# The first two rows of a Sobel stage: row gradients made by VectorE instead of TensorE, and the loads cut to suit

## The chip, the core and the metric

The kernel runs on one core of a Trainium2 chip. Times are device microseconds (us) of that core for one launch of the whole program. A core has a matrix unit (TensorE, PE in the profile, its weight loads PEld), a vector unit (VectorE, DVE), an activation unit (ScalarE, ACT), a general unit (GpSimd, POOL) and a unit that mostly issues DMA transfers (SyncE, SP). ScalarE and GpSimd issue transfers too. Each engine works through its own list of instructions in order, and semaphores tie the lists together.

## The reference, cut to what matters

A batch of 16 images of 3 x 256 x 256 is turned into tokens by a Sobel filter; one attention layer and one feed-forward layer follow. The change touches the first step alone:

```python
kx, ky = _sobel_kernels()   # 3 x 3, per channel
Ix = _dwconv(x, kx)
Iy = _dwconv(x, ky)
G = jnp.hypot(Ix, Iy)
return jnp.sum(G, axis=1)   # over the 3 channels
```

With image rows a, b, c one above the other, and 0, 1, 2 for a shift by that many columns, an output row of `Iy` is `(a0 + 2 a1 + a2) - (c0 + 2 c1 + c2)` and an output row of `Ix` is `(a2 - a0) + 2 (b2 - b0) + (c2 - c0)`. Only their absolute values matter, since `hypot` follows.

## The kernel before, in words

The images go through the core in four groups of four (`GB = 4`). A group fills 128 partitions: 32 partitions for an image, and each partition holds 8 rows of it (`ROWS = 8`), with two more rows below for the filter, in the buffer `img`. "Row r" is thus row r of every partition, 128 x 768 numbers (3 channels x 256 columns), and one instruction on it covers a 32nd of each image. The rows are worked off in pairs (`PAIRS = 4`).

For groups 1 to 3 VectorE makes both gradients itself, in `magnitude_rows`, in between the attention and feed-forward work of the group before. Group 0 has no earlier group beside it. There TensorE makes the gradients, in `stencil(r)`, as sums in its accumulators (`psum`): each term is a matrix product of the identity, or of the identity times -1 or -2 (`ident`, `nident`, `n2ident`), with a row of the image or with a helper row. VectorE makes the helper rows: `edge` = `2 a1 + a0` of an image row, and `lead` = `2 b2 - a0`. `stencil(r)` makes gy from four terms, then gx from five, each term as a product of 512 columns and one of 256; each product of these 4-byte numbers shows in the trace as two instructions, so a term reads "x4". `magnitudes(i)` on ScalarE takes the absolute values of a pair out of the accumulators into `mag_y` and `mag_x`. Then VectorE and ScalarE together run `hypotenuse` on the pair, some fifty VectorE instructions that begin with the maximum and the minimum of the two magnitudes, row by row (f = 0 and 1). Between its steps a hook, `feed`, makes the helper rows of the next pair (`stencil_inputs`), so that TensorE works one pair ahead. `feed` waits for `img_in`, the semaphore of all image rows of the group.

`Chain` (the `u` of the code) orders dependent instructions on VectorE: with `lag=1` an instruction waits until the one before the last is done; `u.all()` waits for all that went before.

The order of the start is written out by hand. SyncE issues the loads of rows 0 to 3 of images 0 and 2, then the table of constants `cst`, then rows 4 to 9 of all images, then weights. ScalarE issues the loads of rows 0 to 3 of images 1 and 3. A load is one transfer per image and channel. VectorE waits for the table, scales the identity by -1 and -2, waits for `img_first` (rows 0 to 3 of all four images), and makes edge 0, edge 2, lead 0, edge 1, edge 3, lead 1. TensorE waits for both scaled identities and for the helper rows it needs. After the last row of group 0 SyncE loads the images of group 1; it knows that by the count of `stencil_psum`, 16 before.

Lines of the kernel before in the profile: L375 issues the image loads and L394 the table; L822 scales the identity; L531 is every `scalar_tensor_tensor` on VectorE (`stt`), L528 every `tensor_tensor` (`tt`), L525 the masking; L1527 is a term of gy and L1539 a term of gx on TensorE; L1266 and L1268 are the absolute values of gy and gx; L1228 is the first square of `hypotenuse` on ScalarE and L1232 the reciprocal root. `edge` and the temporaries `tmp` lie in the big buffers that the profile calls "arena"; `lead` lies in "xT", `nident` and `n2ident` in "onehot".

Of the kernel before, what the change touches and what calls it, by code (L numbers as in the profile page):

```python
# [21 lines left out]
ALU = mybir.AluOpType  # L22
# [99 lines left out]
def tower_kernel(nc, x, cls_tok, w_in, b_qk, b_v, w_out, b_out, w1, conv_w, conv_b, w2, const, out):  # L122
# [9 lines left out]
    with ExitStack() as ctx:  # L132
# [174 lines left out]
        img_first = sem("img_first")  # L307
# [79 lines left out]
        def _(sp):  # L387
# [122 lines left out]
        def _(dve):  # L510
# [296 lines left out]
            def stencil_inputs(rows):  # L807

                for r in rows:
                    if r >= 2:  # L810
                        dve.wait_ge(stencil_psum, 2 * r - 3)
                    edge_row(edge[:, (r + 2) % 4], r + 2).then_inc(edges_out, 1)
                    if r >= 2:
                        dve.wait_ge(stencil_psum, 2 * r - 2)
                    stt(lead[:, r % 2], px(r + 1, 2), 2.0, px(r, 0), ALU.mult, ALU.subtract).then_inc(leads_out, 1)

            def first_group(u):


                dve.wait_ge(table_in, 16)  # L820
                for k, out_ in ((-1.0, nident), (-2.0, n2ident)):
                    v.tensor_scalar(out_, ident, k, None, ALU.mult).then_inc(negated, 1)  # L822
                dve.wait_ge(img_first, FIRST_IN)
                for r in range(2):
                    edge_row(edge[:, r], r).then_inc(edges_out, 1)
                    stencil_inputs([r])
                for i in range(PAIRS):
                    def feed(k, i=i):
                        if k == 1 and i < PAIRS - 1:
                            if i == 0:  # L830
                                dve.wait_ge(img_in, IMG_IN)
                            stencil_inputs((2 * i + 2, 2 * i + 3))
                    hypotenuse(u, 2 * i, i, feed, [mag_x[:, f] for f in range(2)], [mag_y[:, f] for f in range(2)])
# [327 lines left out]
        def _(act):  # L1161
# [96 lines left out]

            def magnitudes(i):

                for f in range(2):
                    r = 2 * i + f
                    if i > 0:
                        act.wait_ge(hisq, 2 * i)
                    act.wait_ge(stencil_psum, 2 * r + 1)
                    s.activation(mag_y[:, f], stencil_sum(2 * r % 4), ACT.Abs).then_inc(mags_y, 1)  # L1266
                    act.wait_ge(stencil_psum, 2 * r + 2)
# [188 lines left out]
            for b in range(1, GB, 2):  # L1456
                load_rows(act, 0, b, 0, 4, img_first)
            act.wait_ge(table_in, 16)
            for i in range(PAIRS):
                magnitudes(i)  # L1460
# [46 lines left out]
        def _(pe):  # L1507
# [7 lines left out]
            def stencil(r):  # L1515
# [3 lines left out]
                if r >= 2:  # L1519
                    pe.wait_ge(mags_y, r - 1)  # L1520
# [8 lines left out]
                pe.wait_ge(leads_out, r + 1)  # L1529
                if r >= 2:  # L1530
                    pe.wait_ge(mags, r - 1)
# [12 lines left out]
            for r in range(ROWS):  # L1544
                if r == 2:
                    pe.wait_ge(img_in, IMG_IN)
# [277 lines left out]
```

## Time and profile before

| | |
|---|---|
| median of 3 runs | 1623.98 us (1623.11 to 1624.61) |
| the profiled execution, its own time | 1622.37 us |
| its span (first to last instruction) | 1620.3 us |
| VectorE busy | 1373.8 us, 85% |
| TensorE busy | 839.6 us, 52% |
| ScalarE busy | 699.8 us, 43% |
| GpSimd busy | 110.1 us, 7% |
| mean granted TensorE clock | 0.707 of full speed |

The span is what the trace covers; the run's own time is 2.1 us longer. In the timelines an entry gives its start and its length in us, and "x3" says that three like instructions were merged into it. What stands in brackets is how long the engine was idle just before it, and who released it.

### The profile page before, as it was taken

Reading aid. Unit: us, or ns where it says so; the run is one execution under the profiler, and the core shown is the slowest. Engines: PE = TensorE matmul, PEld = TensorE weight load, DVE = VectorE, ACT = ScalarE, POOL = GpSimd, SP = SyncE. Lnnn points to the kernel's source line nnn. Section 1 sums busy time; section 2 is a strip of 40 time slices with the busy share of each in tenths; the row PEclk is TensorE's granted clock in tenths of the full one; section 3 lists DMA queues with packets and bytes.
Section 4 is the critical chain, followed back from the end, with each engine's and each line's share of the span. In section 5 each row is a group of like instructions: output and inputs, shape, how many; then the busy total and the mean of one; then the engine's idle time right before and its main releaser. Section 6 shows DMA issues by size and latency. Waiting matters only on the chain.

```text
span 1620.3 us, 12694 instructions
## 1 busy us (share of the span) xinstructions
PE 839.6 (52%) x3318; PEld 655.5 (40%) x3318; DVE 1373.8 (85%) x2145; ACT 699.8 (43%) x1250; POOL 110.1 (7%) x154
## 2 busy tenths in 40 slices
PE   6663200466447743456537754256626764388543
PEld 3332100355336532344426543145525643376433
DVE  1999998899879999899879999899888999722676
ACT  1312332364375544164356553245446653132562
POOL 0000000001101000002101100002010100000000
PEclk9777655766569876667568976577568886577776
DMA  7000500013303510104302610104120300100001
GB/s 192 1 13 14 111 0 0 1 20 52 62 10 59 112 39 1 29 1 71 59 13 41 129 39 1 28 1 72 32 40 10 62 12 28 27 1 0 1 0 27
DMA packets 33421, 57.15 MB, mean 35 GB/s; under 512 B 6410, under 2 KB 23354, under 8 KB 31674
## 3 DMA queue, kind: packets, MB, share of 16 engines
q0 software_dynamic: 21024, 29.11, 11.1%
q1 hardware_dynamic: 12026, 26.31, 7.1%
q10 hardware_dynamic: 288, 0.79, 0.2%
q8 instruction: 32, 0.52, 0.1%
q14 instruction: 51, 0.42, 0.1%
HBM read 22.84 MB, written 4.25 MB: 17 GB/s over the span
## 4 chain that ended last, share of the span: by engine, by line
DVE 30%; issue 26%; ACT 15%; PE 12%; DMA 1%; DVEq 0%; ACTq 0%; SPq 0%
DVE arena L531 9%; DVE arena L528 6%; PE psum L1722 2%; ACT arena L1273 2%; DVE arena L872 2%; PE psum L1672 2%; PE psum L1694 1%; PE psum L1723 1%; PE psum L1576 1%; DVE red L544 1%; PE psum L1758 1%; ACT arena L1409 1%; ACT arena L1169 1%; DVE others L531 1%; ACT zT L1418 1%
## 5 line engine op out<-in xcount | busy, mean ns | idle before, releaser
L528 DVE TENSOR_TENSOR arena<-arena 128x768 f32<-128x768 f32 (+2 forms) x534 | 486.7, 967 | 45.8 <-ACT arena L1207 23.1
L531 DVE SCALAR_TENSOR_TENSOR arena<-arena 128x768 f32<-128x768 f32 (+2 forms) x224 | 201.4, 948 | 0.1
L1590 PE MATMUL psum<-zT,w1q 128*128 128x257 f32 x512 | 150.1, 431 | 41.8 <-ACT wout L1303 25.2
L1590 PEld LDWEIGHTS psum<-zT,w1q 128*128 128x128 f32 x512 | 111.3, 220 | 68.1 <-issue 27.5
L1576 PE MATMUL psum<-gpad,win 128*128 128x257 f32 x288 | 86.0, 442 | 54.9 <-ACT gpad L1285 54.9
L1238 ACT ACTIVATE arena<-arena 128x768 f32<-128x768 int16 x32 | 27.0, 843 | 175.6 <-DVE arena L531 175.2
L1694 PE MATMUL psum<-arena 128*128 128x257 f32 x128 | 50.6, 563 | 86.5 <-ACT arena L1392 65.3
L1576 PEld LDWEIGHTS psum<-gpad,win 128*128 128x128 f32 x288 | 62.6, 223 | 71.9 <-ACT gpad L1285 61.0
L531 DVE SCALAR_TENSOR_TENSOR arena<-img 128x768 f32<-128x768 f32 x88 | 79.5, 949 | 7.0 <-issue 6.4
L504 POOL DMA_DIRECT2D h<-others x60 | 51.7, 862 | 416.6 <-DVE others L531 347.7
L1169 ACT ACTIVATE arena<-arena 128x256 f32<-128x256 f32 x65 | 23.3, 409 | 118.4 <-DVE arena L531 68.2
L1694 PEld LDWEIGHTS psum<-arena 128*128 128x128 f32 x128 | 34.4, 282 | 98.0 <-issue 83.7
L872 DVE TENSOR_REDUCE arena<-arena 128x288 f32<-128x2304 f32 (+1 forms) x16 | 64.6, 4093 | 0.1
L1722 PE MATMUL psum<-arena 128*128 128x64 f32 x256 | 56.5, 361 | 12.3 <-ACT arena L1392 12.3
L476 POOL DMA_DIRECT2D arena<-nrows_mem x18 | 15.6, 902 | 695.1 <-ACT arena L1217 532.1
L1382 ACT ACTIVATE arena<-psum,arena 128x257 f32<-128x257 f32 x64 | 29.5, 474 | 72.5 <-DVE arena L971 72.5
L1292 ACT ACTIVATE xT<-psum,cb 128x257 f32<-128x257 f32 x96 | 43.5, 477 | 36.3 <-PE psum L1576 36.1
L531 DVE SCALAR_TENSOR_TENSOR arena<-arena,others 128x768 f32<-128x768 int16 x64 | 58.2, 950 | 0.0
L1722 PEld LDWEIGHTS psum<-arena 128*128 128x128 f32 x256 | 48.8, 262 | 19.6 <-ACT arena L1392 13.9
L1273 ACT ACTIVATE arena<-xT 128x2048 f32<-128x2048 f32 (+1 forms) x14 | 55.3, 3948 | 0.3
L1647 PE MATMUL psum<-xT,win 128*128 128x257 f32 x128 | 50.2, 559 | 8.4 <-issue 6.9
L531 DVE SCALAR_TENSOR_TENSOR arena<-arena,small 128x256 f32<-128x256 f32 x131 | 53.3, 480 | 0.6
(222 smaller groups left out, 1993.5 us busy)
## 6 DMA issues: line engine op xcount, KB each, us to landing
img<-x SPq DMA_DIRECT2D x36, 258.0 KB, 7.0
h<-others POOLq DMA_DIRECT2D x60, 128.0 KB, 2.7
arena<-nrows_mem POOLq DMA_DIRECT2D x18, 384.0 KB, 4.4
arena<-arena POOLq DMA_DIRECT2D x18, 384.0 KB, 4.1
arena<-img POOLq DMA_DIRECT2D x18, 384.0 KB, 4.9
out<-out SPq DMA_DIRECT2D x16, 256.0 KB
img<-x SPq DMA_DIRECT2D x48, 64.5 KB, 7.7
win<-w_in SPq DMA_DIRECT2D x4, 768.0 KB, 5.4
```

Source lines behind the costliest of these rows:

```text
L504: pool.dma_start(h9[:, row, :], others[:, row % 2, c, :], accum_op=ALU.add).then_inc(row_sums, 16)
L528: return v.tensor_tensor(o, a, b, op)
L531: return v.scalar_tensor_tensor(out=o, in0=a, scalar=s, in1=b, op0=op0, op1=op1)
L872: return v.tensor_reduce(fmax[:, :, bass.ds(b, 1), :].rearrange("p j o r -> p j (o r)"), f4[:, :, :, bass.ds(b, 1), :].rearrange("p t j o ...
L1169: ins = s.activation(ln[1][:, j, :], src(j), ACT.Square)
L1273: s.activation(fb[:, :, 0:ROWS, :], yd[:, :, 1:S].rearrange("p t (r j) -> p t j r", j=ROWS), ACT.Silu)
L1292: s.activation(ydw[:, t, :], (C0, C1, T0, T1)[i % 4][:, 0:S], ACT.Identity, bias=cb[:, t:t + 1]).then_inc(conv_taken, 1)
L1576: ins = mm((C0, C1, T0, T1)[i % 4][:, 0:S], diagonal(t, k), gpad[:, i % 4, k:k + S], start=(k == 0), stop=(k == 2))
L1590: ins = mm((A0, A1, B0, B1)[i % 4][:, 0:S], w1q[:, k, t * P:(t + 1) * P], zT[:, k, b, :], start=(k == 0), stop=(k == DT - 1))
L1647: ins = mm((A0, A1)[t][:, 0:S], win[:, k, D + t * P:D + (t + 1) * P], xT[:, k, b, :], start=(k == 0), stop=(k == DT - 1))
L1694: mm((C0, C1, T0, T1)[hg][:, 0:S], qbd[:, hg // 2, 4 * (hg % 2):4 * (hg % 2) + 4, :].rearrange("p h q -> p (h q)"), kT[:, b % 2, hg // 2, ...
L1722: mm(B1[:, chans], attnT[:, f, m, cols], V[:, b % 2, m, chans], start=(m == 0), stop=False)
```

## The change

For rows 0 and 1 of group 0 the gx of both and the gy of row 1 are made by VectorE in a new function, `first_gradients`, from the image rows in `img` and the helper rows. TensorE makes only gy of row 0, and goes on with row 2 (`stencil(0)` returns after gy). ScalarE takes absolute values in place for what VectorE made (`first_magnitudes`), and scales the identity, which VectorE did before. The loads of rows 0 to 3 are cut in two: rows 0 to 2 of all images first (`img_first`), and row 3 by transfers of its own (`img_second`), after the table on SyncE's queue. `first_gradients` waits for row 3 only where it starts the gx of row 1. The other edits renumber semaphore counts, since TensorE now makes 13 sums in group 0 and not 16.

```diff
             for b in range(0, GB, 2):
-                load_rows(sp, 0, b, 0, 4, img_first)
+                load_rows(sp, 0, b, 0, 3, img_first)
             sp.dma_start(cst[:, :], const).then_inc(table_in, 16)
+            for b in range(0, GB, 2):
+                load_rows(sp, 0, b, 3, 4, img_second)
             for b in range(GB):
                 load_rows(sp, 0, b, 4, ROWS, img_in)
...
                 if first:
-                    sp.wait_ge(stencil_psum, 4 * PAIRS)
+                    sp.wait_ge(stencil_psum, 2 * ROWS - 3)
...
+            def first_gradients(u):
+                F = range(2)
+                dve.wait_ge(img_first, FIRST_IN)
+                for r in (0, 2, 1):
+                    edge_row(edge[:, r], r).then_inc(edges_out, 1)
+                for f in F:
+                    gx, back = tmp[f][0], tmp[f][2]
+                    if f == 1:
+                        dve.wait_ge(img_second, FIRST_IN)
+                    u(stt(gx, px(f + 1, 2), 2.0, px(f, 0), ALU.mult, ALU.subtract))
+                    u(stt(back, px(f + 1, 0), -2.0, px(f, 2), ALU.mult, ALU.add))
+                    u.all()
+                    u(tt(back, back, px(f + 2, 0), ALU.subtract))
+                    u.all()
+                    u(tt(gx, gx, back, ALU.add))
+                    u.all()
+                    tt(gx, gx, px(f + 2, 2), ALU.add).then_inc(first_gx, 1)
+                gy = tmp[1][1]
+                edge_row(edge[:, 3], 3).then_inc(edges_out, 1)
+                dve.wait_ge(edges_out, 4)
+                u(tt(gy, px(1, 2), edge[:, 3], ALU.subtract))
+                u.all()
+                u(tt(gy, gy, edge[:, 1], ALU.add))
+                u.all()
+                tt(gy, gy, px(3, 2), ALU.subtract).then_inc(first_gy, 1)
...
             def first_group(u):
-                dve.wait_ge(table_in, 16)
-                for k, out_ in ((-1.0, nident), (-2.0, n2ident)):
-                    v.tensor_scalar(out_, ident, k, None, ALU.mult).then_inc(negated, 1)
-                dve.wait_ge(img_first, FIRST_IN)
-                for r in range(2):
-                    edge_row(edge[:, r], r).then_inc(edges_out, 1)
-                    stencil_inputs([r])
+                first_gradients(u)
                 for i in range(PAIRS):
                     def feed(k, i=i):
                         if k == 1 and i < PAIRS - 1:
                             if i == 0:
                                 dve.wait_ge(img_in, IMG_IN)
+                                dve.wait_ge(stencil_psum, 1)
+                                dve.wait_ge(first_gy, 1)
                             stencil_inputs((2 * i + 2, 2 * i + 3))
...
+            def first_magnitudes():
+                for f in range(2):
+                    gx = tmp[f][0]
+                    act.wait_ge(first_gx, f + 1)
+                    s.activation(gx, gx, ACT.Abs)
+                    if f == 0:
+                        act.wait_ge(stencil_psum, 1)
+                        s.activation(mag_y[:, 0], stencil_sum(0), ACT.Abs).then_inc(mags, 1)
+                    else:
+                        act.wait_ge(first_gy, 1)
+                        s.activation(tmp[1][1], tmp[1][1], ACT.Abs).then_inc(mags, 1)
...
-            for b in range(1, GB, 2):
-                load_rows(act, 0, b, 0, 4, img_first)
+            for lo, hi_, landed in ((0, 3, img_first), (3, 4, img_second)):
+                for b in range(1, GB, 2):
+                    load_rows(act, 0, b, lo, hi_, landed)
             act.wait_ge(table_in, 16)
+            for k, out_ in ((-1.0, nident), (-2.0, n2ident)):
+                s.activation(out_, ident, ACT.Copy, scale=k).then_inc(negated, 1)
...
                 ins.then_inc(stencil_psum, 1)
-                pe.wait_ge(leads_out, r + 1)
+                if r == 0:
+                    return
+                pe.wait_ge(leads_out, r - 1)
...
             pe.wait_ge(img_first, FIRST_IN)
-            for r in range(ROWS):
-                if r == 2:
-                    pe.wait_ge(img_in, IMG_IN)
+            stencil(0)
+            pe.wait_ge(img_in, IMG_IN)
+            for r in range(2, ROWS):
                 stencil(r)
```

VectorE's list at the start of the program, before. The arena rows from `img` are edges, the xT rows leads, and the two L528 rows that wait for `mags` are the maxima of the first pair:

```order
L822 TENSOR_SCALAR onehot<-cst 128x128 [waits table_in]
L822 TENSOR_SCALAR onehot<-cst 128x128
L531 SCALAR_TENSOR_TENSOR arena<-img 128x768 [waits img_first]
L531 SCALAR_TENSOR_TENSOR arena<-img 128x768
L531 SCALAR_TENSOR_TENSOR xT<-img 128x768
L531 SCALAR_TENSOR_TENSOR arena<-img 128x768 x2
L531 SCALAR_TENSOR_TENSOR xT<-img 128x768
L528 TENSOR_TENSOR arena<-arena 128x768 [waits mags] x2
```

The same place in the changed kernel (its L534 is L531 of before and its L531 is L528). The first two rows hold three edges and the first two instructions of gx of row 0; from "waits img_second" on it is row 1, and from the last L534 on gy of row 1:

```order
L534 SCALAR_TENSOR_TENSOR arena<-img 128x768 [waits img_first]
L534 SCALAR_TENSOR_TENSOR arena<-img 128x768 x4
L531 TENSOR_TENSOR arena<-arena,img 128x768 [waits vstep_g0]
L531 TENSOR_TENSOR arena<-arena 128x768 [waits vstep_g0]
L531 TENSOR_TENSOR arena<-arena,img 128x768 [waits vstep_g0]
L534 SCALAR_TENSOR_TENSOR arena<-img 128x768 [waits img_second]
L534 SCALAR_TENSOR_TENSOR arena<-img 128x768 [waits vstep_g0]
L531 TENSOR_TENSOR arena<-arena,img 128x768 [waits vstep_g0]
L531 TENSOR_TENSOR arena<-arena 128x768 [waits vstep_g0]
L531 TENSOR_TENSOR arena<-arena,img 128x768 [waits vstep_g0]
L534 SCALAR_TENSOR_TENSOR arena<-img 128x768
L531 TENSOR_TENSOR arena<-img,arena 128x768 [waits edges_out]
```

Two more instructions of gy follow, each with a wait for `vstep_g0`, and then the two maxima. Before them stand 17 instructions where 8 stood, two leads and both scalings have gone, and no instruction waits for the table.

ScalarE's list at the start, before:

```order
L375 DMA img<-x 32x1032 x6
L1266 ACT_TABLE_LOAD [waits stencil_psum]
L1266 ACTIVATE arena<-psum 128x768 [waits table_in]
L1268 ACTIVATE arena<-psum 128x768 [waits stencil_psum]
L1266 ACTIVATE arena<-psum 128x768 [waits stencil_psum]
L1268 ACTIVATE arena<-psum 128x768 [waits stencil_psum]
```

And in the changed kernel, where the last four rows are the absolute values of gx and gy of row 0, then of row 1:

```order
L376 DMA img<-x 32x774 x6
L376 DMA img<-x 32x258 x6
L1505 ACT_TABLE_LOAD
L1505 ACTIVATE onehot<-cst 128x128 [waits table_in]
L1505 ACTIVATE onehot<-cst 128x128
L1296 ACTIVATE arena<-arena 128x768 [waits first_gx]
L1299 ACTIVATE arena<-psum 128x768 [waits stencil_psum]
L1296 ACTIVATE arena<-arena 128x768 [waits first_gx]
L1302 ACTIVATE arena<-arena 128x768 [waits first_gy]
```

Six more transfers are issued ahead, the scaling of the identity comes in, and three of the four absolute values now read what VectorE made; the count of table loads stays the same.

## Rows read from the trace of the kernel before

**Rows 1.** Page, busy time of each engine.

```profile
PE 839.6 (52%) x3318; PEld 655.5 (40%) x3318; DVE 1373.8 (85%) x2145; ACT 699.8 (43%) x1250; POOL 110.1 (7%) x154
```

**Rows 2.** Timeline of VectorE: start, length, idle before it.

```profile
11.17 0.36 DVE L822 TENSOR_SCALAR onehot<-cst 128x128 f32<-128x128 f32 x2 [11.17 <-DMA cst<-const]
11.45 1.82 DVE L531 SCALAR_TENSOR_TENSOR arena<-img 128x768 f32<-128x768 f32 x2
...
27.87 0.96 DVE L528 TENSOR_TENSOR arena<-arena 128x768 f32<-128x768 f32 x1 [11.13 <-ACT arena L1268]
39.48 2.70 DVE L528 TENSOR_TENSOR arena<-arena 128x768 f32<-128x768 f32 x3 [10.65 <-ACT arena L1268]
...
44.77 0.95 DVE L531 SCALAR_TENSOR_TENSOR arena<-img 128x768 f32<-128x768 f32 x1
...
88.77 1.83 DVE L528 TENSOR_TENSOR arena<-arena 128x768 f32<-128x768 f32 x2
...
138.95 1.82 DVE L528 TENSOR_TENSOR arena<-arena 128x768 f32<-128x768 f32 x2
```

**Rows 3.** Timeline of TensorE and ScalarE, first two pairs.

```profile
13.41 2.90 PE L1527 MATMUL psum<-img,cst 128*128 128x512 f32 x4 [13.41 <-DVE arena L531]
20.62 1.28 ACT L1266 ACT_TABLE_LOAD   x1 [20.62 <-PE psum L1527]
38.64 0.81 ACT L1268 ACTIVATE arena<-psum 128x768 f32<-128x768 f32 x1 [5.64 <-PE psum L1539]
40.47 0.84 ACT L1228 ACTIVATE arena<-arena 128x768 f32<-128x768 f32 x1 [0.29 <-DVE arena L528]
45.82 2.90 PE L1527 MATMUL psum<-img,cst 128*128 128x512 f32 x4 [7.22 <-issue]
70.41 1.45 PE L1539 MATMUL psum<-img,cst 128*128 128x512 f32 x4
```

**Rows 4.** Busy time by stretch: PE, PEld, DVE, ACT, POOL, PEclk, DMA, GB/s.

```profile
0.00:5.00 5.00, 0.00 (x0) 0.00 (x0) 0.00 (x0) 0.00 (x0) 1.47 (x8) 1.00 0.65 149
5.00:10.00 5.00, 0.00 (x0) 0.00 (x0) 0.00 (x0) 0.00 (x0) 0.00 (x0) 1.00 1.03 228
45.80:51.00 5.20, 5.18 (x8) 2.86 (x9) 5.20 (x7) 0.00 (x0) 0.00 (x0) 0.50 0.01 3
51.00:72.00 21.00, 20.86 (x65) 11.94 (x63) 20.96 (x25) 3.44 (x5) 0.00 (x0) 1.00 0.00 0
290.00:735.00 445.00, 237.91 (x963) 194.97 (x963) 408.37 (x623) 211.77 (x385) 34.28 (x44) 0.70 0.20 36
1180.00:1620.00 440.00, 250.78 (x1068) 202.72 (x1067) 312.76 (x551) 203.66 (x384) 16.89 (x24) 0.74 0.09 17
```

**Rows 5.** L375 on SyncE, issued 2.1 to 3.0, then 4.4 to 4.9, 14.7 to 15.2.

```profile
L375 SPq DMA_DIRECT2D img<-x x3: 421/422/422, 2.1 to 3.0; - x3
DMA to landing us min/median/max: 5.1/6.2/6.8
...
DMA to landing us min/median/max: 8.1/8.1/8.1
...
DMA to landing us min/median/max: 7.5/7.6/7.6
```

**Rows 6.** L375, ScalarE's image loads issued 2.1 to 3.1.

```profile
L375 ACTq DMA_DIRECT2D img<-x x3: 443/443/443, 2.1 to 3.1; - x3
DMA to landing us min/median/max: 5.9/6.5/7.2
```

**Rows 7.** Timeline of SyncE's queue, image loads after the table.

```profile
3.98 11.64 SPq L375 DMA_DIRECT2D img<-x  x24
```

**Rows 8.** Chain that ended last, in order of time, two waits on the instruction before.

```profile
260.25 3.66 DVE arena L531 x9
263.94 3.66 DVE arena L531 x9
```

**Rows 9.** Page, the chain that ended last, shares by engine.

```profile
DVE 30%; issue 26%; ACT 15%; PE 12%; DMA 1%; DVEq 0%; ACTq 0%; SPq 0%
```

More of the change, by code:

```diff
@@ L306, in tower_kernel @@
         img_in = sem("img_in")
-        img_first = sem("img_first")
+        img_first = sem("img_first"); img_second = sem("img_second")
+        first_gy = sem("first_gy"); first_gx = sem("first_gx")
         hypots = sem("hypots"); row_sums = sem("row_sums"); rows_done = sem("rows_done")
@@ L831, in feed @@
                                 dve.wait_ge(img_in, IMG_IN)
+                                dve.wait_ge(stencil_psum, 1)
+                                dve.wait_ge(first_gy, 1)
                             stencil_inputs((2 * i + 2, 2 * i + 3))
-                    hypotenuse(u, 2 * i, i, feed, [mag_x[:, f] for f in range(2)], [mag_y[:, f] for f in range(2)])
+                    if i == 0:
+                        gx, gy = [t[0] for t in tmp], [mag_y[:, 0], tmp[1][1]]
+                    else:
+                        gx, gy = [[m[:, f] for f in range(2)] for m in (mag_x, mag_y)]
+                    hypotenuse(u, 2 * i, i, feed, gx, gy)
                 dve.wait_ge(hypots, ROWS)
@@ L1262, in magnitudes @@
                     r = 2 * i + f
-                    if i > 0:
-                        act.wait_ge(hisq, 2 * i)
-                    act.wait_ge(stencil_psum, 2 * r + 1)
+                    act.wait_ge(hisq, 2 * i)
+                    act.wait_ge(stencil_psum, 2 * r - 2)
                     s.activation(mag_y[:, f], stencil_sum(2 * r % 4), ACT.Abs).then_inc(mags_y, 1)
-                    act.wait_ge(stencil_psum, 2 * r + 2)
+                    act.wait_ge(stencil_psum, 2 * r - 1)
                     s.activation(mag_x[:, f], stencil_sum((2 * r + 1) % 4), ACT.Abs).then_inc(mags, 1)
@@ L1454, in slots_1 @@
                 return slot
-            for b in range(1, GB, 2):
-                load_rows(act, 0, b, 0, 4, img_first)
+            for lo, hi_, landed in ((0, 3, img_first), (3, 4, img_second)):
+                for b in range(1, GB, 2):
+                    load_rows(act, 0, b, lo, hi_, landed)
             act.wait_ge(table_in, 16)
+            for k, out_ in ((-1.0, nident), (-2.0, n2ident)):
+                s.activation(out_, ident, ACT.Copy, scale=k).then_inc(negated, 1)
             for i in range(PAIRS):
-                magnitudes(i)
+                if i == 0:
+                    first_magnitudes()
+                else:
+                    magnitudes(i)
                 hypotenuse(2 * i, lambda k: weight_means() if i == PAIRS - 1 and k == 4 else None)
@@ L1518, in stencil @@
                 pe.wait_ge(edges_out, EDGE_ORDER.index(r + 2) + 1)
-                if r >= 2:
-                    pe.wait_ge(mags_y, r - 1)
+                if r == 2:
+                    pe.wait_ge(mags, 1)
+                if r >= 4:
+                    pe.wait_ge(mags_y, r - 3)
                 for weight, first, last, src in (
```

11 lines of the change are left out of this document (6 added, 5 removed).

## The prediction

> **What bounds the kernel now.** I read the busy times of the page first: VectorE works 85% of the span, TensorE 52%, ScalarE 43% [rows 1]. So the question is where VectorE's 15% of idle time lies, and whether the change touches any of it. The timeline of VectorE at the start answers that [rows 2]. The engine waits 11.17 us for the table of constants, works through six helper rows, waits 11.13 us for the first magnitude (gx of row 0) and, after one maximum, 10.65 us for the one of row 1. Both releasers are ScalarE's absolute value of gx. From 39.48 on it is never held again in group 0: the next pair begins at 88.77 and the one after it at 138.95, 50.2 us apart, as long as the instructions in them take.
>
> The timeline of TensorE and ScalarE says why [rows 3]. TensorE starts at 13.41, has the first gy done when ScalarE begins on it at 20.62, and the last gx of row 1 at 38.64. VectorE stands behind four sums made one after the other, and ScalarE is only the last link. In the second pair it is the reverse. TensorE starts at 45.82, once edge 4 (44.77 plus 0.95) is there, and ends its last term at 71.86. VectorE comes back for the result at 88.77. So only the first pair waits for TensorE, and a microsecond by which VectorE gets earlier to the second maximum of that pair is a microsecond for all that follows.
>
> **The change part by part.** The measure is the start of the second maximum, 39.48 before. I build its new time.
>
> *The first instruction.* The wait for the table goes to ScalarE. What is late next is `img_first`. The last of the twelve transfers of before were issued at 3.0 and 3.1 and landed 6.8 and 7.2 us later, at 9.8 and 10.3 [rows 5, 6]. How much of this rows 0 to 2 save I get from the rate. The twelve carried 12 x 129 KB = 1.585 MB. 149 GB/s over the first 5 us are 0.745 MB, the other 0.84 MB at 228 GB/s take 3.7 us [rows 4]: 8.7 us, and 10.3 was measured, so 1.6 us went to other transfers served in between and to the finish. Now it is three quarters, 1.189 MB: 0.745 MB, then 0.444 MB in 1.95 us, 6.95, and three quarters of the 1.6 us, 8.15. With the start of the instruction I take 8.3. Ends: 7.0, if nothing comes in between, and 10.3, if it lands no earlier than before.
>
> *VectorE's own work.* 17 instructions of 128x768 stand ahead of the first maximum. Two in a row take 1.82 us and one 0.95, so one that isn't held starts 0.87 after the one before [rows 2]. One that waits for the instruction right before it doesn't show in this shape. The nearest row is a group of nine that takes 3.66 from 260.25; the next, which needs it, starts at 263.94, 0.03 after its end [rows 8]. So a held start is 0.95 + 0.03 = 0.98. Held are nine: three in each gx (the subtraction, the sum, the last addition) and all three of gy, the first behind edge 3. From the first to the last of the 17 are 16 starts, 9 x 0.98 + 7 x 0.87 = 14.91. The last, which finishes gy of row 1, starts at 8.3 + 14.9 = 23.2. All at 0.87 would be 1.0 us less, all at 0.98 0.8 more.
>
> The Trainium skill (VectorE: DVE Perf Modes, section "The DRAIN you can't avoid") says that the next instruction doesn't start until the pipe is empty, and that a semaphore after each costs nothing extra. By it all starts would be alike, and the sum would move to one of the two ends just named; the row that starts 0.87 after one of 0.95 speaks against the first half.
>
> *The last link.* gy of row 1 ends at 23.2 + 0.95, ScalarE takes its absolute value (0.84, the row of the like square, 40.47 in [rows 3]), and with 0.03 for each handover the second maximum starts at 25.06. The first maximum could start at 23.2 + 0.87 = 24.1 and be done at 25.03, so about 0.1 us is all that VectorE waits there.
>
> *What must be hidden.* Gy of row 0 has to be out before 24.1. Even if TensorE starts no earlier than before, at 13.41, ScalarE can begin on it at 20.62 [rows 3] and is done in 0.81, at 21.4. The scaling of the identity, now on ScalarE behind the table (11.17 at the latest), has no row. The nearest small ones are VectorE's pair of 0.36, and a whole 128x768 activation of 0.84 is above any 128x128 one, so two take 0.36 to 1.7: at 12.9 latest. The table load of 1.28 waits for nothing in the new list, and runs after the issues. So TensorE starts within about half a microsecond of before or earlier, and I count nothing; cover is 2.6 us. ScalarE's absolute values of gx lie in gaps between VectorE's results.
>
> Row 3 is wanted at the ninth instruction: 8.3 + 3 x 0.87 + 0.87 + 3 x 0.98 + 0.87 = 15.6. SyncE issues it between 4.0 and 6.7 (24 issues took 11.64, 0.485 each [rows 7]). All bytes issued up to then are the same 1.96 MB as before, and the two transfers issued at 4.4 and 4.9, which had at least those bytes ahead of them, landed 8.1 us later, at 13.0 [rows 5]. Cover: 2.6 us.
>
> All other rows (`img_in`) are wanted at the first `feed`, 5.3 us after the second maximum (44.77 against 39.48 [rows 2]): 30.4. The last was issued at 15.2 and landed at 22.8 [rows 5]. Six more issues ahead of it make 2.9 us: 25.7, or 26.2 with the 8.1 above. Cover: 4.2 us. What is queued behind that wait is the helper rows of pair 1, and behind these TensorE.
>
> *The sum.* 39.48 - 25.06 = 14.4 us earlier at the second maximum. From there to 88.77 nothing is removed or added, since row 2 on TensorE still begins 1.05 us after edge 4 starts. Checked by VectorE's account: idle falls by 11.17 - 8.3 = 2.9, by 11.13 and by 10.65 less 0.1, 24.6 in all, and 11 instructions come in (17 for 6) while the two scalings go. That is 9 x 0.98 + 2 x 0.87 - 0.36 = 10.2. The difference is 14.4. SyncE's load for group 1 waits for the same event as before, at the same distance, and nothing later hangs on a fixed time: the last weights are issued 3 us later and used 150 us later. The profiled execution would take 1622.4 - 14.4 = 1608.0. It lies 1.6 below the median of the runs, which becomes 1624.0 - 14.4 = 1609.6. The likeliest case's own range comes from the start (7.0 to 10.3, +1.3 and -2.0) and the held starts (+1.0 to -0.8): 11.6 to 16.7 us gained, 1607.3 to 1612.4.
>
> **The rivals.**
>
> *The loads decide.* For: VectorE's first wait is a transfer now and will be one after, and twelve small transfers come in. Against: the loads of rows 8 and 9, half as big as the others, didn't lower the rate. If each row-3 transfer costs as much as one of 129 KB (0.58 us at 228 GB/s), twelve take 7.0, the table 1.7, and row 3 lands at 8.2 + 8.7 = 16.9: 1.3 us late, 13.1 gained, inside the range above. With 10.3 for rows 0 to 2 on top, row 3 comes at 19.0, wanted at 17.6: 1.4 late, 14.4 - 2.0 - 1.4 = 11.0 gained, 1613.0.
>
> The Trainium skill (DMA: Bandwidth & Descriptors, section "Bandwidth") calls transfers under 64 KB dominated by their descriptors, and gives 0.95 us for one of 64 KB. Row 3 is made of transfers of 32 KB. As an estimate from that page twelve in a row would be 11.4 us, row 3 at 19.6, 4 us late, and the time 1613.6. No transfer so small bears on anything in the trace of before.
>
> *TensorE stays slow in group 0.* After its pause TensorE runs at half clock, 1.2 GHz: 0.50 for 5.2 us, then 1.00, 2.4 GHz [rows 4]. It now has one sum of work ahead of its pause where it had four. If it stayed at 1.2 GHz, a pair would take 5.3 + 2 x 20.7 = 46.7 instead of 26.0. With 0.8 for the absolute value and 6.3 to its next start, a pair lasts 53.9 and not 50.2, and 3.7 us are lost in each of three: 1613.3 for one, 1620.7 for all. Against it: before, it paused 24 us ahead of the third pair and was back at full clock within 5 us.
>
> *The first wait isn't the path.* If VectorE's time at the start were given back at the next meeting with other engines, as 4.2 us of cover on `img_in` gone and more, the time would be near 1624. Against it stands that from the second maximum on the order of the work is that of before.
>
> *The other sign.* TensorE's part in the chain that ended last is 12% of the span [rows 9], 194 us. Its mean clock differs from stage to stage, 0.70 against 0.74 [rows 4]. If moving the stages against the clock's changes lowered it there, the 14.4 us would be gone once 7.4% were added to these 194. With twice the difference of the two rows, 0.08 of 0.70 or 11.4%, it would be 22 us: 1609.6 + 22 = 1631.7, slower than before. Against it: every stage follows its own work and moves as a whole.
>
> **How the numbers follow.** The forecast, 11.6 to 16.7 gained, gets 0.82. The loads late beyond it, around 1613, 0.07. TensorE slow in one to three pairs, 1613 to 1621, 0.05. Gain lost, near 1624, 0.04. Slower, 0.02. That a measurement can tell from no change is about 0.2%, 3.2 us. Faster by more takes the forecast, the loads and most of the TensorE case: 0.94. Within it are the lost gain and all three slow pairs: 0.04. Slower 0.02. The predicted time is 1609.6. The range is 1607.0 to 1614.0; it takes in the loads case and a single slow pair.
>
> **What would show it.** In the profile after, VectorE's first row should be an L534 at about 8.3 with the wait on `img`, not on `cst`. Its next idle time over 0.3 us should come only after group 0. The first `tensor_tensor` that needs a magnitude should start near 24.1, the second near 25.1, and the next pair near 74.3. TensorE should begin at 13.4 or before, pause after 7 us, and begin row 2 near 31.4. It is wrong if the ninth instruction waits for row 3, if edge 4 waits for `img_in`, if ScalarE reaches gy of row 0 after 23, or if pairs in group 0 lie more than 50.3 apart. A gain at 74.3 that is gone at the end would put the fault in the later stages.

## The result, and the profile after

The changed kernel takes 1609.49 us (median of 4 runs, 1607.81 to 1610.47) against 1623.55 (4 runs, 1622.52 to 1624.61). The ratio is 0.9911, with a 95% interval of 0.9897 to 0.9925: 12 to 17 us faster. The profiled execution took 1608.93 and has a span of 1607.1, 13.2 less than before. One run of the kernel before, beside the first experiments, was disturbed as a whole (2702.73 us) and counts in no number here.

The timeline of VectorE in the changed kernel, from the start to the first pair's maxima, the beginnings of the next two pairs, and the next instruction with an idle time over 0.3 us before it. Columns are as in [rows 2]: start, length, and in brackets the idle time and its releaser.

```profile
8.61 4.43 DVE L534 SCALAR_TENSOR_TENSOR arena<-img 128x768 f32<-128x768 f32 x5 [8.61 <-DMA img<-x]
13.15 0.96 DVE L531 TENSOR_TENSOR arena<-arena,img 128x768 f32<-128x768 f32 x1
14.22 0.96 DVE L531 TENSOR_TENSOR arena<-arena 128x768 f32<-128x768 f32 x1
15.28 0.96 DVE L531 TENSOR_TENSOR arena<-arena,img 128x768 f32<-128x768 f32 x1
16.16 1.82 DVE L534 SCALAR_TENSOR_TENSOR arena<-img 128x768 f32<-128x768 f32 x2
...
21.08 0.95 DVE L534 SCALAR_TENSOR_TENSOR arena<-img 128x768 f32<-128x768 f32 x1
22.07 0.96 DVE L531 TENSOR_TENSOR arena<-img,arena 128x768 f32<-128x768 f32 x1
23.13 0.96 DVE L531 TENSOR_TENSOR arena<-arena 128x768 f32<-128x768 f32 x1
24.20 0.96 DVE L531 TENSOR_TENSOR arena<-arena,img 128x768 f32<-128x768 f32 x1
25.07 3.69 DVE L531 TENSOR_TENSOR arena<-arena 128x768 f32<-128x768 f32 x4
...
31.35 0.95 DVE L534 SCALAR_TENSOR_TENSOR arena<-img 128x768 f32<-128x768 f32 x1
...
75.37 0.96 DVE L531 TENSOR_TENSOR arena<-arena 128x768 f32<-128x768 f32 x1
...
125.53 0.96 DVE L531 TENSOR_TENSOR arena<-arena 128x768 f32<-128x768 f32 x1
...
235.50 2.55 DVE L547 TENSOR_REDUCE red<-arena 128x72 f32<-128x2304 f32 x1 [2.63 <-ACT arena L1200]
```

Three idle times of [rows 2], 11.17, 11.13 and 10.65 us, have become one of 8.61. Four maxima and minima run on without a break from 25.07 (four at 0.87 apart would take 3.57, they take 3.69). The next pair starts at 75.37 against 88.77, 13.4 us earlier, and the one after it 50.2 us later, as before. The fourth pair begins at 175.71, so the idle time at 235.50 lies behind group 0.

The timeline of ScalarE and TensorE in the same stretch, which answers to [rows 3]:

```profile
6.49 1.28 ACT L1505 ACT_TABLE_LOAD   x1 [6.49 <-issue]
9.64 0.51 ACT L1505 ACTIVATE onehot<-cst 128x128 f32<-128x128 f32 x2 [1.87 <-DMA cst<-const]
17.43 0.81 ACT L1299 ACTIVATE arena<-psum 128x768 f32<-128x768 f32 x1 [0.31 <-PE psum L1579]
25.19 0.84 ACT L1302 ACTIVATE arena<-arena 128x768 f32<-128x768 f32 x1 [3.15 <-DVE arena L531]
10.59 2.90 PE L1579 MATMUL psum<-img,cst 128*128 128x512 f32 x4 [10.59 <-DVE arena L534]
32.41 2.90 PE L1579 MATMUL psum<-img,cst 128*128 128x512 f32 x4 [15.01 <-DVE arena L534]
```

TensorE starts at 10.59, and ScalarE has its only sum from 17.43 to 18.24. VectorE's first maximum, which wants it, starts 6.8 us after that. The last link is ScalarE's absolute value of gy of row 1, 25.19 to 26.03, right behind VectorE's last instruction.

The image loads of the changed kernel: SyncE's rows 0 to 2 issued at 2.6 and 3.1, ScalarE's at the same times (both rows merge the neighbour before or after), SyncE's last two of row 3, and its last ones of rows 8 and 9:

```profile
L376 SPq DMA_DIRECT2D img<-x x2: 422/422/423, 2.6 to 3.1; - x2
DMA to landing us min/median/max: 4.6/4.8/5.0
...
L376 ACTq DMA_DIRECT2D img<-x x2: 442/442/442, 2.6 to 3.1; - x2
DMA to landing us min/median/max: 5.0/5.2/5.5
...
L376 SPq DMA_DIRECT2D img<-x x2: 421/422/422, 6.0 to 6.5; - x2
DMA to landing us min/median/max: 6.1/6.3/6.5
...
L376 SPq DMA_DIRECT2D img<-x x3: 421/422/425, 16.7 to 17.6; - x3
DMA to landing us min/median/max: 5.2/5.3/5.4
```

Rows 0 to 2 are in at 3.1 + 5.5 = 8.6, row 3 at 6.5 + 6.5 = 13.0 (wanted at 16.16, the start of the ninth instruction), the last row at 17.6 + 5.4 = 23.0 (wanted at 31.35).

### The profile page after: what moved, and what is told of

Its sections match the earlier page's. It is cut to its first block, busy times and chain, and to the rows that moved or that the text cites. A ratio compares the mean times of both kernels' runs of the same rounds, so it can differ in the third digit from the quotient of the medians.

```text
span 1607.1 us, 12610 instructions
## 1 busy us (share of the span) xinstructions
PE 814.8 (51%) x3262; PEld 639.7 (40%) x3262; DVE 1383.6 (86%) x2154; ACT 700.1 (44%) x1252; POOL 110.1 (7%) x154
## 4 chain that ended last, share of the span: by engine, by line
DVE 31%; issue 27%; ACT 15%; PE 12%; DMA 1%; DVEq 0%; SPq 0%; ACTq 0%
DVE arena L534 9%; DVE arena L531 6%; PE psum L1776 2%; ACT arena L1317 2%; DVE arena L903 2%; PE psum L1726 2%; PE psum L1630 1%; PE psum L1777 1%; PE psum L1812 1%; DVE red L547 1%; ACT arena L1453 1%; ACT arena L1200 1%; PE psum L1748 1%; DVE others L534 1%; ACT zT L1462 1%
## 5 line engine op out<-in xcount | busy, mean ns | idle before, releaser
L531 DVE TENSOR_TENSOR arena<-arena 128x768 f32<-128x768 f32 (+2 forms) x537 | 489.6, 967 | 24.8 <-ACT arena L1238 23.1
L534 DVE SCALAR_TENSOR_TENSOR arena<-arena 128x768 f32<-128x768 f32 (+2 forms) x224 | 201.5, 949 | 0.1
L534 DVE SCALAR_TENSOR_TENSOR arena<-img 128x768 f32<-128x768 f32 x92 | 83.1, 950 | 16.4 <-DMA img<-x 8.6
L534 DVE SCALAR_TENSOR_TENSOR arena<-arena,others 128x768 f32<-128x768 int16 x64 | 58.2, 949 | 0.0
L1726 PE MATMUL psum<-onehot,arena 128*128 128x128 f32 x128 | 24.2, 366 | 62.9 <-DVE arena L979 62.9
L531 DVE TENSOR_TENSOR arena<-arena,img 128x768 f32<-128x768 f32 x59 | 53.9, 950 | 0.5
```

The source lines that it names most:

```text
L531: return v.tensor_tensor(o, a, b, op)
L534: return v.scalar_tensor_tensor(out=o, in0=a, scalar=s, in1=b, op0=op0, op1=op1)
L1726: ins = mm(C0[:, t * P:(t + 1) * P], y_row(j)[:, t * P:(t + 1) * P], rhs, start=(j == 0), stop=(j == ROWS))
```

## The experiments

The runs were made in three batches, each on another chip and each with runs of the kernel before beside it; the ratios are to these. The first batch (start_only, gradients_only, one_wait, gy1_tensor) has 16 of them with a median of 1624.10 us, the second (eight_more, after_again, interleaved, prewarmed) 9 with 1623.70, the third (gy1_again, prewarmed_again) 9 with 1623.81. The milestone of most experiments is "the next pair": VectorE's first maximum of the second pair, 88.77 before and 75.37 in the changed kernel.

**start_only** does the edits to the start alone (cut; VectorE and TensorE also wait for `img_second` ahead of row 1):

```diff
-                load_rows(sp, 0, b, 0, 4, img_first)
+                load_rows(sp, 0, b, 0, 3, img_first)
...
+                load_rows(sp, 0, b, 3, 4, img_second)
...
-                    v.tensor_scalar(out_, ident, k, None, ALU.mult).then_inc(negated, 1)
+                s.activation(out_, ident, ACT.Copy, scale=k).then_inc(negated, 1)
```

> Only the edits to the start: rows 0 to 2 first, row 3 apart, ScalarE scales the identity; TensorE still makes all sums of rows 0 and 1. Theory (the first pair waits for TensorE alone): VectorE's first row comes at 8.6 instead of 11.17 and that by itself is worth nothing, but TensorE starts at 10.6 instead of 13.41, so the second maximum starts at 36.7 and not 39.48, the next pair at 86.0 and not 88.77, and the time falls by 2.8 us. Rival (the early start is worth nothing without the gradients on VectorE): second maximum at 39.5, time as before.

It took 1621.55 us (11 runs), ratio 0.9980 (0.9971 to 0.9989). The first two terms of TensorE's first sum, and VectorE's second maximum:

```profile
10.99 2.90 PE L1531 MATMUL psum<-img,cst 128*128 128x512 f32 x4 [10.99 <-DVE arena L533]
13.68 2.62 PE L1531 MATMUL psum<-arena,onehot 128*128 128x512 f32 x4
...
37.83 2.70 DVE L530 TENSOR_TENSOR arena<-arena 128x768 f32<-128x768 f32 x3 [10.65 <-ACT arena L1269]
```

The theory holds in its kind. VectorE's first instruction comes at 9.02 and that is worth nothing: it waits 0.81 us for row 3, and then 11.00 and 10.65 us for the magnitudes, where it waited 11.13 and 10.65. TensorE's earlier start is worth something. TensorE started 2.4 us earlier, and 1.65 of it arrived at the second maximum (39.48 to 37.83), since its second term took 2.62 us, where it took 1.85 before (16.10 to 17.95): it worked longer at the slow rate. That difference isn't a property of the edits. Two profiled executions of the changed kernel itself, the first one and then after_again, differ by more in the same term:

```profile
13.28 1.53 PE L1579 MATMUL psum<-arena,onehot 128*128 128x512 f32 x4
```

```profile
13.51 2.65 PE L1579 MATMUL psum<-arena,onehot 128*128 128x512 f32 x4
```

Between the medians the edits are worth 2.6 us (1624.10 to 1621.55), 1.8 to 4.7 by the interval of the ratio, which agrees with the 2.8 expected. The rival, a time as before, falls.

**gradients_only** has VectorE's gradients with the loads and the scaling as before:

```diff
+                dve.wait_ge(table_in, 16)
+                for k, out_ in ((-1.0, nident), (-2.0, n2ident)):
+                    v.tensor_scalar(out_, ident, k, None, ALU.mult).then_inc(negated, 1)
                 dve.wait_ge(img_first, FIRST_IN)
```

> Only the move of the gradients to VectorE: loads of rows 0 to 3 in one piece and the identity scaled by VectorE, as before. Theory (after the change the path to the second maximum is VectorE's own list from its first instruction on): everything is late by its later start, 11.45 against 8.6, so the next pair starts at 75.4 + 2.8 = 78.2 and the time is 2.8 us above the changed kernel, about 10.6 below before. Rival (the gain is the removed TensorE work and the start edits only move idle time): next pair at 75.4, time as the changed kernel.

It took 1614.35 us (5 runs), ratio 0.9933 (0.9919 to 0.9946). VectorE's first rows and its next pair:

```profile
12.61 0.36 DVE L824 TENSOR_SCALAR onehot<-cst 128x128 f32<-128x128 f32 x2 [12.61 <-DMA cst<-const]
12.88 4.43 DVE L532 SCALAR_TENSOR_TENSOR arena<-img 128x768 f32<-128x768 f32 x5
...
79.64 0.96 DVE L529 TENSOR_TENSOR arena<-arena 128x768 f32<-128x768 f32 x1
```

The first edge starts 4.27 us later than in the changed kernel (12.88 against 8.61), since the table happened to land 1.4 us later in this run than in that of before, and the next pair starts 4.27 us later (79.64 against 75.37). The theory holds to the hundredth: the start now reaches the next pair one to one. Had the table landed as in the trace of before (11.45 for the first edge), it would be 2.8 us. The time is 4.9 us above the changed kernel's median of 1609.49 (1613.3 against 1609.3 by the means, 4.0), on another chip and with runs that lie 3.3 us apart, so how much of it is the late table can't be told. The rival, a time like the changed kernel's, falls. In the traces the edits to the start are worth 1.6 us at the next pair without VectorE's gradients (88.77 to 87.14) and 4.3 with them, but a late table makes 1.4 of the 4.3 and a long slow stretch of TensorE lowers the 1.6, so the two are closer than they look.

**eight_more** lengthens VectorE's list by a known amount:

```diff
+                for k in range(8):
+                    u(edge_row(tmp[k // 4][3 + k % 4], 0))
                 for r in (0, 2, 1):
```

> The changed kernel with eight more edge instructions of VectorE (128x768, results not used) ahead of its first one. Theory (the path to the second maximum is VectorE's own list, and all that follows keeps its distance): 8 x 0.87 = 7.0 us more at the second maximum (33.0), at the next pair (82.3) and in the time, 1616.5. Rival (a later meeting with another engine takes up what the start gains or loses): the 7.0 us stand at 82.3 and shrink by more than 2 us until the end, 1614 or less.

ScalarE ends the last absolute value, which releases the second maximum, at 32.86, and the next pair starts at 82.19, 6.8 us later than in the changed kernel (6.9 if the loads' 0.1 us is taken off). The time is 1615.28 us (5 runs, 1615.19 to 1618.04), against 1609.06 for the changed kernel beside it: 6.2 us more, and 6.9 by the means (1616.0 and 1609.1). The rival, more than 2 us taken up on the way, isn't seen, though runs that spread over 3 us can't rule out a smaller part.

**after_again** is the changed kernel once more.

> The changed kernel once more, on the chip of the three runs beside it, to have more of its times: 1608 to 1611 us, second maximum near 26.0, next pair near 75.4. Theory (what scatters the runs by 2 to 3 us is TensorE's granted clock in the attention stages of the four groups, not the start): the first pairs agree with the first profile to 0.5 us even if the time doesn't.

It took 1609.06 us (5 runs, 1607.76 to 1610.96), ratio 0.9910 (0.9897 to 0.9924). The second maximum started near 26.3 and the next pair at 75.58, against 75.37. So the start agrees to 0.2 us while the times spread over 3. That the granted clock makes the spread isn't borne out: over the nine runs of this kernel, these five and the first four, mean clock and time hardly go together (correlation 0.07).

**one_wait** takes away the second of two waits in the first gradients (one of six places is shown, the others are alike):

```diff
+                def one(ins):
+                    u.n += 1
+                    ins.then_inc(u.sem, 1)
...
-                    u(tt(back, back, px(f + 2, 0), ALU.subtract))
+                    one(tt(back, back, px(f + 2, 0), ALU.subtract))
                     u.all()
```

> The changed kernel, but a dependent instruction of the first gradients stands behind one wait, for the instruction right before it, where it stood behind two (one for the instruction before the last, then one for the last). Theory (the second wait costs VectorE's sequencer 0.07 us each time): held starts fall from 1.06 to 0.99, as the one behind edge 3 that has a single wait, and the second maximum starts 0.5 us earlier, at 25.5. Rival (a tensor_tensor behind a tensor_tensor that it needs costs 1.06 in any case): nothing moves.

VectorE's first held instructions, and the maxima:

```profile
13.19 0.96 DVE L531 TENSOR_TENSOR arena<-arena,img 128x768 f32<-128x768 f32 x1
14.18 0.96 DVE L531 TENSOR_TENSOR arena<-arena 128x768 f32<-128x768 f32 x1
15.17 0.96 DVE L531 TENSOR_TENSOR arena<-arena,img 128x768 f32<-128x768 f32 x1
...
24.61 3.69 DVE L531 TENSOR_TENSOR arena<-arena 128x768 f32<-128x768 f32 x4
```

Held starts are 0.99 apart and not 1.06. From the first instruction to the first maximum it is 15.89 us (8.72 to 24.61) where it was 16.46 (8.61 to 25.07), and the next pair starts at 74.92, 0.45 us before the changed kernel's. The theory holds. Its one run, 1606.00 us, is in line with that, and more can't be said from a single one.

**gy1_tensor** leaves gy of row 1 to TensorE, with edge 3 made ahead of the gx of row 1:

```diff
-                    else:
-                        act.wait_ge(first_gy, 1)
-                        s.activation(tmp[1][1], tmp[1][1], ACT.Abs).then_inc(mags, 1)
...
-                if r == 0:
+                if r < 2:
                     return
...
             stencil(0)
+            pe.wait_ge(img_second, FIRST_IN)
+            stencil(1)
             pe.wait_ge(img_in, IMG_IN)
```

> The changed kernel, but gy of row 1 is left to TensorE; both gx stay on VectorE, with edge 3 made ahead of the gx of row 1. Theory (VectorE's list is now longer than TensorE's, which ends its one sum at 17.4): TensorE ends the second gy at 22.6, VectorE loses three held instructions (3.2 us), the first maximum starts at 22.0 and the second at about 23.7, when ScalarE has taken the second gy, instead of 26.0: 2.3 us faster than the changed kernel. Rival (each sum left to TensorE holds up the pair, as before the change): second maximum at 26 or later, no gain or a loss.

VectorE's maxima and its next pair:

```profile
21.84 0.95 DVE L531 TENSOR_TENSOR arena<-arena 128x768 f32<-128x768 f32 x1
23.55 2.69 DVE L531 TENSOR_TENSOR arena<-arena 128x768 f32<-128x768 f32 x3 [0.77 <-ACT arena L1290]
...
72.87 1.83 DVE L531 TENSOR_TENSOR arena<-arena 128x768 f32<-128x768 f32 x2
```

In this trace the pair is as the theory had it: second maximum at 23.55, next pair 2.5 us before the changed kernel's; the rival, 26 or later, falls. The time is not: 1610.08 us (6 runs, 1605.18 to 1612.77), and the profiled one took 1612.76. The start of the token selection in the third group, in the changed kernel and then in gy1_tensor, shows that the lead was gone by then:

```profile
1026.01 0.41 DVE L956 MAX8 best<-nrows_mem 4x8 f32<-4x257 f32 x1
```

```profile
1030.12 0.41 DVE L948 MAX8 best<-nrows_mem 4x8 f32<-4x257 f32 x1
```

A lead of 2.5 us at 73 has become a lag of 4.1. The busy time by stretch shows TensorE's granted clock (the first number after POOL's) a hundredth lower in both middle stages, for the changed kernel:

```profile
290.00:735.00 445.00, 241.67 (x1001) 197.92 (x1002) 409.48 (x614) 211.91 (x391) 40.06 (x50) 0.70 0.23 40
735.00:1180.00 445.00, 235.14 (x937) 189.07 (x936) 402.81 (x605) 206.84 (x382) 43.31 (x57) 0.69 0.23 41
```

and for gy1_tensor:

```profile
290.00:735.00 445.00, 242.34 (x986) 198.41 (x986) 405.12 (x607) 210.27 (x384) 39.64 (x49) 0.69 0.22 40
735.00:1180.00 445.00, 237.12 (x941) 192.03 (x941) 402.04 (x603) 205.94 (x375) 42.96 (x55) 0.68 0.24 42
```

These hundredths don't explain it alone: in prewarmed_again (below) the same stretches have 0.69 and 0.68 as well, and its selection in the third group starts at 1025.67.

**gy1_again** asks whether that is a property of this start.

> gy1_tensor once more. Its first six runs lay between 1605.2 and 1612.8 us with a granted clock of 0.710 to 0.697, though its first pair was 2.5 us ahead of the changed kernel's. Theory (the scatter comes from TensorE's clock in the later stages and is no property of this start): the median comes out near 1609.3 - 2.5 = 1606.8, and the runs with the lower mean clock are the longer ones. Rival (this start puts the later stages at a worse place against the clock's changes): again 1610 or more.

It took 1608.33 us (5 runs, 1607.18 to 1612.21). TensorE's second term, and VectorE's second maximum and next pair in its profiled run:

```profile
13.14 2.77 PE L1567 MATMUL psum<-arena,onehot 128*128 128x512 f32 x4
...
24.75 2.69 DVE L531 TENSOR_TENSOR arena<-arena 128x768 f32<-128x768 f32 x3 [1.99 <-ACT arena L1290]
...
74.05 3.56 DVE L531 TENSOR_TENSOR arena<-arena 128x768 f32<-128x768 f32 x4
```

The same kernel started its second maximum at 23.55 in one execution and at 24.75 in the other. VectorE's own list was the same to 0.03 us, but TensorE's second term took 2.77 us and not 1.78, the third 1.72 and not 1.45, and with TensorE at the end of the path that reaches the pair. The lead on the changed kernel at the next pair is 2.5 us in one trace and 1.3 in the other, so the 1606.8 expected stood on the better of the two.

All eleven runs together have a median of 1609.19; nine of the changed kernel, 1609.06. In the eleven the longer runs are mostly those with the lower mean clock (correlation -0.73; 1605.18 at 0.710, 1612.77 at 0.697), as the theory has it. But a median near 1606.8 didn't come, so a lead of 1.3 to 2.5 us in the first pair is worth nothing that these runs can tell, and the rival isn't excluded.

**interleaved** also takes the gx of both rows in turn:

```diff
+                for f in F:
+                    u(tt(tmp[f][2], tmp[f][2], px(f + 2, 0), ALU.subtract))
+                for f in F:
+                    u(tt(tmp[f][0], tmp[f][0], tmp[f][2], ALU.add))
```

> gy of row 1 left to TensorE, and the instructions of both gx taken in turn, row 0 and row 1, so that none waits for the one right before it. Theory (held starts and VectorE's count of instructions set the pair until TensorE's second gy does): VectorE would be ready for the second maximum at 21.9, TensorE ends its second gy at 22.6, so the second maximum starts at 23.4 instead of 26.0, the next pair at 72.8, and the time is 2.6 us below the changed kernel. Rival (the lost interleaving is worth more than the end of gy on TensorE): second maximum before 22.5.

It took 1607.37 us (4 runs), ratio 0.9896 (0.9881 to 0.9911). Its loads landed late in the profiled run (first instruction at 9.34, not 8.6), TensorE started at 11.79, and the second maximum at 24.66. From TensorE's start to the second maximum it is 12.9 us, where 10.5 to 23.4 had been expected, the same 12.9: TensorE's second gy is the end of the path now, and VectorE waits 1.37 us for it. VectorE's 14 instructions of this start come 0.87 us apart throughout, so taking the rows in turn removes the holding as meant, and the rival, a second maximum before 22.5, falls. The next pair starts at 73.96, where 72.8 had been expected.

**prewarmed** keeps TensorE busy with zeros until its first term:

```diff
+            pe.wait_ge(gpad_zero, 1)
+            for k in range(12):
+                mm(psum[:, 3072:3328], gpad[:, 0, 0:P], gpad[:, 1, 0:256], start=True, stop=True)
             pe.wait_ge(negated, 2)
```

> As interleaved, and TensorE runs twelve products of zeros, 256 columns each, from about 2 us on, whose results are not used, until its first real term. Theory (TensorE's first sum is long because the engine stood still before it and works at 1.2 GHz for the first 3 to 5 us): it now works at 2.4 GHz from its first term, both gy end 1.5 to 2 us earlier, at about 20.9, the second maximum starts at 22.0, the next pair at 71.3, 4 us before the changed kernel. Rival (the first sum is long for its operands' sake): gy ends at 22.6 as in interleaved.

TensorE's first rows, then VectorE's second maximum and next pair:

```profile
1.76 7.78 PE L1587 MATMUL psum<-gpad 128*128 128x256 f32 x24 [1.76 <-POOL gpad L466]
10.58 1.53 PE L1568 MATMUL psum<-img,cst 128*128 128x512 f32 x4 [1.04 <-DVE arena L534]
11.94 1.45 PE L1568 MATMUL psum<-arena,onehot 128*128 128x512 f32 x4
...
23.02 2.69 DVE L531 TENSOR_TENSOR arena<-arena 128x768 f32<-128x768 f32 x3 [0.47 <-ACT arena L1291]
...
72.33 0.96 DVE L531 TENSOR_TENSOR arena<-arena 128x768 f32<-128x768 f32 x1
```

The first term takes 1.53 us where it took 2.90, so its operands were not the reason; the standing still was. In prewarmed_again it takes 1.56, and the spread of gy1_tensor's two traces in the second term doesn't appear (1.45 in both). The second gy is ready at 21.2. The second maximum comes at 23.02, a microsecond later than expected, because ScalarE, which takes both gx and both gy in a fixed order, has four absolute values in a row from 20.02 on, when the gx of row 0 is ready. The time is 1606.28 us (4 runs, 1605.44 to 1608.67), ratio 0.9890 (0.9875 to 0.9905).

**prewarmed_again** repeats it.

> prewarmed once more: next pair at 72.3, median 1606.3, about 3.0 us below the changed kernel, if what the start gains is carried to the end. A median of 1608 or more would say that its first four runs were lucky.

Its next pair starts at 72.19. It took 1607.18 us (4 runs), ratio 0.9894 (0.9879 to 0.9909), under the 1608 that would have spoken of luck. The eight runs together have a median of 1606.96, 2.1 us below the changed kernel's 1609.06 over nine, for a next pair 3.0 to 3.2 us earlier. It is the fastest version tried in several runs; since the kernels' own runs spread over 3 us, the 2 us are likely and not certain. Letting ScalarE take gy of row 0 ahead of the gx wasn't tried.

**Where a lead of the start is lost.** The start of the token selection in each group (its first MAX8) lets one follow a lead through the program. All starts are of the profiled executions, in us:

| | next pair | group 1 | group 2 | group 3 | group 4 | span |
|---|---|---|---|---|---|---|
| before | 88.77 | 296.49 | 667.83 | 1039.47 | 1399.46 | 1620.3 |
| changed | 75.37 | 283.44 | 653.63 | 1026.01 | 1386.02 | 1607.1 |
| after_again | 75.58 | 283.10 | 655.58 | 1027.26 | 1387.34 | 1605.9 |
| gy1_tensor | 72.87 | 280.39 | 656.14 | 1030.12 | 1390.05 | 1610.9 |
| gy1_again | 74.05 | 281.84 | 654.54 | 1026.01 | 1385.63 | 1606.5 |
| prewarmed | 72.33 | 280.02 | 654.69 | 1025.85 | 1385.73 | 1606.9 |
| prewarmed_again | 72.19 | 279.91 | 653.80 | 1025.67 | 1385.54 | 1606.7 |

The 13 us of the change stay at every milestone. The leads of 1.3 to 3.2 us are all still there at the first selection. At the second they can't be told from the scatter: between these two milestones the two executions of the changed kernel move 2.3 us apart themselves. What makes this scatter in the second group isn't shown.

## Why the prediction was right, point by point

**The place.** Right: the first pair alone waited for TensorE. Two of VectorE's three idle times went and the third fell to 8.61 us; nothing in group 0 took their place. The pairs still lie 50.2 us apart.

**The first instruction.** 8.3 was forecast from the rate, 8.61 came. Over all profiled runs that load rows 0 to 2 first it lay between 8.46 and 9.34, and the wait is for the last transfer of rows 0 to 2, as stated.

**VectorE's own work.** Here a term was mis-sized. 14.91 us was forecast from the first to the last of the 17, 15.59 came (8.61 to 24.20). Starts that aren't held are 0.87 apart, as taken. Of the nine held ones only that behind edge 3 came at 0.99, near the 0.98 that [rows 8] gave; the other eight came at 1.06 or 1.07. one_wait gives the reason. They stand behind two waits, the one that `u` adds for the instruction before the last and the one of `u.all()`, and with one wait they come at 0.99. The row I drew on has one wait, which is why it gave 0.98. The Trainium skill (VectorE: DVE Perf Modes, section "The DRAIN you can't avoid") says, of a chain of copies, that a semaphore after each instruction costs nothing extra. That doesn't carry over to these instructions: a wait for the one right before costs 0.12 us and two waits 0.19, on 0.87.

**The last link.** The second maximum: 25.06 forecast, about 26.0 measured (ScalarE is done at 25.19 + 0.84 = 26.03; the merged row of four begins at 25.07). Of the microsecond 0.3 is the start, 0.7 the double waits. The gain at the next pair was 13.4 and not 14.4.

**What was to be hidden.** All of it was, with more room than counted: gy of row 0 by 6.8 us (5.7 in after_again, where TensorE's slow stretch was longer), row 3 by 3.2 where 2.6 had been counted, the last rows by 8.3. The rival of the loads falls: twelve transfers of 32 KB took no longer to land (6.5 us at most) than the earlier ones of 129 KB [rows 5]. The prediction's estimate from the Trainium skill (DMA: Bandwidth & Descriptors, section "Bandwidth"), whose figure is for transfers issued by GpSimd, had row 3 land at 19.6; it was in at 13.0. Two loads of the kernel before with at least as many bytes ahead of them were in at 13.0 as well [rows 5], so with a queue of loads standing in both traces the size of one doesn't show.

**TensorE's clock in group 0.** After a pause of 15 us it began row 2 at a granted clock of 0.50, which is 1.2 GHz, was at 1.00 (2.4 GHz) from 37.5 on, and ended the pair's last term at 58.30, 17 us before VectorE came back for it. So this rival falls too. The traces show a smaller effect that I hadn't counted: at the start of the program TensorE's slow stretch isn't of the same length in two executions of the same kernel. In the changed kernel it has cover, in gy1_tensor it hasn't.

**The sum.** 14.4 us forecast; 13.4 in the profiled executions (1622.37 to 1608.93), 14.1 between the medians of four runs each (1623.55 to 1609.49). That 1609.6 met 1609.49 so closely is partly luck: the sum was 1.0 too high, the medians moved 0.7 further than the two profiled runs, and the median of before that I subtracted from was of three runs and 0.4 higher than that of four.

**Carried to the end.** Shown to the size of the scatter: 13.4 us at the next pair and 13.2 in the span, and in eight_more 6.8 at the next pair and 6.2 in the medians. For leads of 1.3 to 3.2 us it isn't shown in the traces: from the second selection on they can't be told from the scatter, and only the medians of prewarmed keep 2.1 us. What in the later stages moves a run by some microseconds stays open. The mean clock goes with it in that kernel's eleven runs, but hardly in the changed kernel's nine (correlation 0.07) and prewarmed's eight (-0.16), and no run changed the clock in those stages alone.

## What to carry to other kernels

Look for the one place where the busiest engine waits, and count the new path to it instruction by instruction, telling starts that are held from those that aren't; a helper that adds a second wait to each costs as well. An edit can act through another engine than the one it is made for: in start_only VectorE's earlier start was worth nothing, since it waited for TensorE later, but TensorE's was worth something; once that wait had gone, VectorE's start reached the next pair one to one. Before trusting a gain of 2 us in a program of 1600, profile the same kernel twice and compare a milestone near the edit with the end. While VectorE's own list leads to it, the milestone agreed to 0.2 us; with TensorE's first sums at the end of the path it moved by 1.2, and the times spread over 3 to 8 us in any case.

## What the runs showed of the hardware

- A VectorE instruction of 128x768 starts 0.87 us after the one before when nothing holds it, 0.99 behind one wait for it, 1.06 behind two.
- TensorE's first term after standing still took 2.90 us, and 1.53 when it had worked on zeros for 7.8 us until 1.0 us before, with the granted clock given as 1.00 in both stretches: the clock column doesn't show this slow stretch. It does show the one after a pause of 15 us (0.50).
- How long TensorE stays slow at the start differs between executions of one kernel: its second term took 1.53 and 2.65 us in two profiles of the changed kernel, 1.78 and 2.77 in two of gy1_tensor, and 1.45 in both of prewarmed.
